# An input quantizer whose small steps are done once for four batches

## The reference

```
x = (h - mean) / sqrt(var + 1e-5)              # 2560 rows of 512
chunks of 64 rows:                             # 10 for each batch, 40 in all
ch_bias = (max + min) / 2                      # per chunk and channel
xz = x - ch_bias
tmax = max |xz| of the chunk; cmax = max |xz| of the chunk and channel
idx = sum(cmax > tmax / 2**(7..1))             # 8 scale groups of channels
scale = tmax / 2**(7 - idx) / 7
result = clip(round(xz / scale), -8, 7) * scale
q, k, v = result @ W_quantized + ch_bias @ W + b
```

## Time and profile before

| | |
|---|---|
| time, median of 3 runs | 1826.13 us (1821.69 to 1829.0) |
| the profiled execution | 1825.29 us, of which the span of the trace is 1823.5 us |
| busy shares in the span | PE 74%, DVE 72%, ACT 42%, POOL 27% |
| TensorE's mean granted clock | 0.864 of full speed |
| stretch of the normalisation and quantizer | 166.9 to 292.6 us |

### The profile page before, as it was taken

One profiled execution on the slowest core, in us unless ns is written; L12 is line 12 of the kernel. 1 busy time (PEld: TensorE's weight loads), 2 busy tenths in 40 slices (PEclk: granted clock), 3 DMA queues, 4 the chain that ended last, 5 costly groups with the idle time before them and its releaser, 6 DMA issues. The chain is left out here.

```text
span 1823.5 us, 30220 instructions
## 1 busy us (share of the span) xinstructions
PE 1341.7 (74%) x10126; PEld 766.5 (42%) x10245; DVE 1309.7 (72%) x2158; ACT 767.5 (42%) x1459; POOL 500.1 (27%) x313
## 2 busy tenths in 40 slices
PE   0366117864989999999999941426469999999993
PEld 0335103321334444344444410113457777777772
DVE  7975898996878888788888819999644444444441
ACT  4565001330667777677777740002213333333331
POOL 4000113764134343343300002123113233333321
PEclk9976559785899999999999975667579999999997
DMA  4002002769457767667564443326458887878865
GB/s 146 1 0 84 0 0 78 222 210 210 148 168 200 209 181 210 183 185 209 162 123 77 107 137 82 68 34 177 152 211 283 269 289 258 264 266 289 260 166 138
DMA packets 115662, 294.31 MB, mean 161 GB/s; under 512 B 19772, under 2 KB 54332, under 8 KB 105446
## 3 DMA queue, kind: packets, MB, share of 16 engines
q1 hardware_dynamic: 89262, 205.79, 36.9%
q0 software_dynamic: 25280, 84.95, 17.7%
q10 hardware_dynamic: 1056, 2.79, 0.5%
HBM read 206.39 MB, written 92.16 MB: 164 GB/s over the span
## 5 line engine op out<-in xcount | busy, mean ns | idle before, releaser
L1292 ACT ACTIVATE pT<-p 128x512 f32<-128x512 f32 x800 | 421.6, 607 | 170.8 <-PE p L1194 97.5
L1266 DVE TENSOR_REDUCE mxa<-p 128x1 f32<-128x512 f32 x640 | 409.3, 682 | 99.0 <-PE p L1176 98.8
L1176 PE MATMUL p<-ks,qs 96*128 96x512 bf16 x640 | 253.8, 399 | 34.7 <-DMA vs<-d_v 27.1
L1194 PE MATMUL p<-qs,ks 128*128 128x512 bf16 x560 | 215.2, 384 | 26.3 <-DMA qs<-nmT 13.0
L1212 PE MATMUL p<-pT,vs 128*32 128x128 f32 (+1 forms) x2560 | 207.1, 441 | 1.4 <-ACT pT L1292 1.4
L1812 PE MATMUL p<-x,w 128*128 128x256 bf16 x1728 | 191.6, 273 | 0.0
L1812 PEld LDWEIGHTS p<-x,w 128*128 128x128 bf16 x1728 | 169.1, 98 | 23.4
L1783 POOL DMA_INDIRECT d_acc<-yo,slot_row x54 | 86.5, 1602 | 311.2 <-DMA d_acc<-yo,slot_row 260.6
L1891 DVE SCALAR_TENSOR_TENSOR sg<-p,b,sg 128x256 f32<-128x256 f32 x108 | 52.3, 484 | 118.3 <-ACT sg L1857 118.2
L1212 PEld LDWEIGHTS p<-pT,vs 128*32 128x32 f32 x2560 | 67.0, 109 | 153.2 <-issue 109.9
L1147 POOL CAST xT<-xT 128x2048 bf16<-128x2048 f32 x24 | 45.3, 1887 | 300.7 <-PE p L1212 288.5
(11 more groups left out here) (333 smaller groups left out, 2117.8 us busy)
## 6 DMA issues: line engine op xcount, KB each, us to landing
w<-d_w SPq DMA_DIRECT2D x18, 2048.0 KB, 8.5
d_w<-xT POOLq DMA_DIRECT2D x24, 1024.0 KB, 6.4
shared<-d_w SPq DMA_DIRECT2D x9, 2048.0 KB, 8.3
w<-d_w SPq DMA_DIRECT2D x18, 1024.0 KB, 7.2
xT<-in_w1T POOLq DMA_DIRECT2D x16, 1024.0 KB, 10.6
qs<-d_q SPq DMA_DIRECT2D x192, 80.0 KB, 3.6
ks<-d_k SPq DMA_DIRECT2D x192, 80.0 KB, 3.7
d_v<-xT SPq DMA_DIRECT2D x20, 512.0 KB, 4.4
```

Source lines behind the costliest of these rows:

```text
L1176: mm = pe.matmul(out, qs[u][0:STACK, h, q], ks[u][0:STACK, h, 0:512], start=True, stop=True)
L1194: mm = pe.matmul(out, ks[u][:, h, k], qs[u][:, h, 0:512], start=True, stop=True)
L1266: dve.tensor_reduce(mxa[u][:, h, qt:qt + 1], bank, AX.X, ALU.max, negate=True).then_inc(s_mfree, 1)
L1292: act.activation(dst, ps[:, second_bank(c, s)], ACT.Exp).then_inc(s_p, 1)
```

## The change

A new class `GroupQuantizer` takes the place of `Quantizer` in `project`. The ORDER list goes. Now:

- DVE takes the statistics of all four batches' first tiles in a row, one square root serves all 20 tiles, and 20 tiles are normalised one after the other. PE's transposes use four PSUM banks.
- `extremes` (DVE, for each batch) does maximum, minimum and the negated chunk bias. GpSimd adds it to batches 0, 1 and 2 (`centre`), ACT to batch 3 in 40 activations of 128x64 with the bias as a per-partition operand.
- `scales` (DVE, once) does the small operations on 128x160 values for all 40 chunks, with one round trip over PE. The scale group no longer comes from the loop of seven comparisons: it comes from the exponent and mantissa bits of the maxima, taken as integers.
- `apply` (DVE, for each batch) multiplies, rounds, and clamps; the last pass is four instructions of 128x640 instead of one of 128x2560.
- the token scales are copied by ACT, and the bias products use the negated bias, which the following operation subtracts.

```
+    def extremes(self, dve, chain, b, x):
+        at = self.columns(b)
+        chain(dve.tensor_reduce(self.mx[:, :, at], self.chunks(x), AX.X, ALU.max))
+        chain(dve.tensor_reduce(self.mn[:, :, at], self.chunks(x), AX.X, ALU.min))
+        chain(dve.tensor_tensor(self.ncb[:, :, at], self.mx[:, :, at], self.mn[:, :, at], ALU.add))
+        dve.tensor_scalar(self.ncb[:, :, at], self.ncb[:, :, at], -0.5, None, ALU.mult).then_inc(self.bias_ready, 1)
+    def scales(self, dve, chain, k, ready):
+        chain(dve.tensor_tensor(self.mx[:], self.mx[:], self.ncb[:], ALU.add))
+        chain(dve.tensor_tensor(self.mn[:], self.mn[:], self.ncb[:], ALU.add))
+        chain(dve.scalar_tensor_tensor(self.u[:], self.mn[:], -1.0, self.mx[:], ALU.mult, ALU.max))
+        dve.tensor_reduce(self.c1[:], self.u[:].rearrange("p i c -> p c i"), AX.X, ALU.max).then_inc(self.cmax_ready, 1)
+        dve.wait_ge(self.cmax_turned, k + 1)
+        chain(dve.tensor_reduce(self.tm[:], self.ps_t[0:n, 0:P], AX.X, ALU.max))
+        dve.tensor_scalar(self.diag[:], self.ident[0:n, 0:n], self.tm[:], None, ALU.mult).then_inc(self.tmax_ready, 1)
+        dve.wait_ge(self.tmax_spread, k + 1)
+        chain(dve.tensor_copy(self.tmb[:], self.ps_b[:, 0:n]))
+        chain(dve.scalar_tensor_tensor(self.up[:], wide(self.tmb[:]), 2.0 ** -7, self.u[:], ALU.mult, ALU.max))
+        chain(dve.tensor_scalar(bits(self.tf[:]), bits(self.tmb[:]), MANTISSA, UNITY, ALU.bitwise_and, ALU.bitwise_or))
+        chain(dve.tensor_scalar(bits(self.F[:]), bits(self.up[:]), MANTISSA, UNITY, ALU.bitwise_and, ALU.bitwise_or))
+        chain(dve.tensor_scalar(bits(self.tp[:]), bits(self.tmb[:]), EXPONENT, None, ALU.bitwise_and))
+        chain(dve.tensor_scalar(bits(self.s[:]), bits(self.up[:]), EXPONENT, None, ALU.bitwise_and))
+        chain(dve.tensor_scalar(bits(self.tp[:]), bits(self.tp[:]), -1.0, float(2 * UNITY), ALU.mult, ALU.add))
+        chain(dve.tensor_tensor(self.F[:], self.F[:], wide(self.tf[:]), ALU.is_gt))
+        chain(dve.scalar_tensor_tensor(self.F[:], self.F[:], 1.0, self.s[:], ALU.add, ALU.mult))
+        chain(dve.tensor_tensor(self.F[:], self.F[:], wide(self.tp[:]), ALU.mult))
+        chain(dve.tensor_tensor(self.s[:], self.F[:], wide(self.tmb[:]), ALU.mult))
+        chain(dve.tensor_scalar(self.s[:], self.s[:], 1.0 / QMAX, 1e-9, ALU.mult, ALU.max))
+        dve.tensor_scalar(self.gb[:], self.tmb[:], 1.0 / QMAX, 1e-9, ALU.mult, ALU.max).then_inc(ready, 1)
+        dve.wait_ge(ready, k + 1)
+        chain(dve.reciprocal(self.rg[:], self.gb[:]))
+        chain(dve.tensor_tensor(self.F[:], self.s[:], wide(self.rg[:]), ALU.mult))
+        chain(dve.reciprocal(self.s[:], self.s[:]))
+    def apply(self, dve, chain, b, x, out, done):
+        chain(dve.tensor_tensor(x4, x4, self.spread(self.s[:, :, at]), ALU.mult))
+        chain(dve.tensor_scalar(flat, flat, MAGIC, MAGIC, ALU.add, ALU.subtract))
+        for i in range(IT):
+            ins = dve.scalar_tensor_tensor(o4[:, i], x4[:, i], QMAX, self.F[:, i, at].unsqueeze(2).broadcast_to(
+                [P, self.NB, CHUNK]), ALU.min, ALU.mult)
+        ins.then_inc(done, 1)
...
@@ ACT: after one square root and 20 copies
+            act.wait_ge(quant.bias_ready, B)
+            for i in range(IT):
+                for c in range(NB):
+                    x = xT[:, LAST, i, c * CHUNK:(c + 1) * CHUNK]
+                    ins = act.activation(x, x, ACT.Identity, bias=quant.ncb[:, i, k:k + 1])
+            ins.then_inc(s_centred[1], 1)
+            act.wait_ge(s_scales, 1)
+            for half in range(2):
+                act.copy(gtok[rows], g[rows, :, half]).then_inc(s_gtok, 1)
@@ GpSimd
-            for b in range(B):
-                quant.gpsimd(pool, b, xT[:, b])
+            for b in range(LAST):
+                pool.wait_ge(quant.bias_ready, b + 1)
+                quant.centre(pool, b, xT[:, b]).then_inc(s_centred[0], 1)
@@ DVE
+            for b in range(B):
+                ins = dve.bn_stats(bst[:, b], hs[:, b * COMPS])
+            chain(ins)
+            for b in range(B):
+                ins = dve.bn_aggr(mv[:, b * COMPS], bst[:, b])
+            chain(ins)
+            dve.tensor_scalar(mv[:, :, 1], mv[:, :, 1], EPS_LN, None, ALU.add).then_inc(s_var, 1)
+            dve.wait_ge(s_std, 1)
+            chain(dve.reciprocal(sd[:], sd[:]))
+            for r in range(TILES):
+                b, c = divmod(r, COMPS)
+                if b >= 2 and c == 0:
+                    dve.wait_ge(s_turn, (b - 1) * COMPS)
+                dve.tensor_scalar(xn[:, b % 2, c], hs[:, r], mv[:, r, 0:1], sd[:, r:r + 1],
+                                  ALU.subtract, ALU.mult).then_inc(s_xn, 1)
+            for b in range(B):
+                dve.wait_ge(s_xT, (b + 1) * COMPS)
+                quant.extremes(dve, chain, b, xT[:, b])
+            dve.wait_ge(quant.bias_ready, B)
+            quant.scales(dve, chain, 0, s_scales)
+            for b in range(B):
+                if b < LAST:
+                    dve.wait_ge(s_centred[0], b + 1)
+                else:
+                    dve.wait_ge(s_centred[1], 1)
+                quant.apply(dve, chain, b, xT[:, b], qF[:, b], s_q)
...
+            dve.wait_ge(s_gtok, 2)
```

More of the change, by code:

```diff
@@ L743, in vector, with __init__, sb, sem @@
         dve.scalar_tensor_tensor(o3, x3, QMAX, wide(self.F[:]), ALU.min, ALU.mult).then_inc(done, 1)
-    def token_scales(self, dve, chain):
-        g = self.gb[:].rearrange("p b (t h) -> p (b t) h", h=2)
-        for half in range(2):
-            rows = slice(half * CHUNK, (half + 1) * CHUNK)
-            chain(dve.tensor_copy(self.gtok[rows], g[rows, :, half]))
+class GroupQuantizer:
+    NB = T // CHUNK
+    def __init__(self, nc, ctx, ident, ones, ps_t, ps_b, tag, batches):
+        def sb(name, shape, dt=F32):
+            return ctx.enter_context(nc.sbuf_tensor(f"{name}{tag}", shape, dt))
+        def sem(name):
+            return ctx.enter_context(nc.semaphore(f"{name}{tag}"))
+        self.n = n = batches * self.NB
+        self.ident, self.ones, self.ps_t, self.ps_b = ident, ones, ps_t, ps_b
+        self.mx, self.mn, self.u, self.up, self.F, self.s, self.ncb = (sb(x, [P, IT, n]) for x in (
+            "qmx", "qmn", "qu", "qup", "qF", "qs", "qncb"))
+        self.c1, self.tmb, self.tf, self.tp, self.gb, self.rg = (sb(x, [P, n]) for x in (
+            "qc1", "qtmb", "qtf", "qtp", "qgb", "qrg"))
+        self.tm, self.diag = sb("qtm", [n, 1]), sb("qdiag", [n, n])
+        self.bias_ready, self.cmax_ready, self.cmax_turned, self.tmax_ready, self.tmax_spread = (sem(x) for x in (
+            "chunk_bias_ready", "chunk_max_ready", "chunk_max_turned", "tmax_ready", "tmax_spread"))
+    def tensor(self, pe, k):
+        n = self.n
+        pe.wait_ge(self.cmax_ready, k + 1)
+        pe.transpose(self.ps_t[0:n, 0:P], self.c1[:], self.ident[:]).then_inc(self.cmax_turned, 1)
+        pe.wait_ge(self.tmax_ready, k + 1)
+        pe.matmul(self.ps_b[:, 0:n], self.ones[0:n, :], self.diag[:], start=True, stop=True).then_inc(self.tmax_spread, 1)
+    def columns(self, b):
+        return slice(b * self.NB, (b + 1) * self.NB)
+    def spread(self, ap):
+        return ap.unsqueeze(3).broadcast_to([P, IT, self.NB, CHUNK])
+    def chunks(self, x):
+        return x.rearrange("p i (c t) -> p i c t", c=self.NB)
+    def centre(self, eng, b, x):
+        return eng.tensor_tensor(self.chunks(x), self.chunks(x), self.spread(self.ncb[:, :, self.columns(b)]), ALU.add)
+    def extremes(self, dve, chain, b, x):
[5 more added lines that the diff above has]
+    def scales(self, dve, chain, k, ready):
+        n = self.n
+        EXPONENT, MANTISSA, UNITY = 0x7F800000, 0x007FFFFF, 0x3F800000
+        def bits(ap):
+            return ap.bitcast(I32)
+        def wide(ap):
+            return ap.unsqueeze(1).broadcast_to([P, IT, n])
+        chain(dve.tensor_tensor(self.mx[:], self.mx[:], self.ncb[:], ALU.add))
[24 more added lines that the diff above has]
+    def apply(self, dve, chain, b, x, out, done):
+        at = self.columns(b)
+        x4 = self.chunks(x)
+        flat = x.rearrange("p i t -> p (i t)")
+        chain(dve.tensor_tensor(x4, x4, self.spread(self.s[:, :, at]), ALU.mult))
+        chain(dve.tensor_scalar(flat, flat, MAGIC, MAGIC, ALU.add, ALU.subtract))
+        o4 = self.chunks(out)
+        for i in range(IT):
+            ins = dve.scalar_tensor_tensor(o4[:, i], x4[:, i], QMAX, self.F[:, i, at].unsqueeze(2).broadcast_to(
+                [P, self.NB, CHUNK]), ALU.min, ALU.mult)
+        ins.then_inc(done, 1)
@@ L956, in _ @@
                 dve.wait_ge(s_bmm, n + 1)
[L957 removed]
+                dve.tensor_tensor(Bt[:, n], bias[:, n], ps[0:NCH, n], ALU.subtract).then_inc(s_bt, 1)
             for n in range(2):
```

73 lines of the change are left out of this document (28 added, 45 removed).

## The result

The changed kernel takes 1786.34 us (median of 5 runs, 1773.3 to 1788.99), the kernel before 1826.13 in the same comparison: a ratio of 0.977, with a 95% interval of 0.975 to 0.979. Two further sets of five gave 1782.58 (1773.83 to 1786.19; ratio 0.977, 0.974 to 0.979) and 1779.89 (1776.56 to 1783.6; ratio 0.974, 0.971 to 0.977). The forecast was 1781 in a range of 1775 to 1797. The profiled execution of the changed kernel is the quickest of its set: 1773.3 us, span 1771.3.

The account below looks back on a forecast made before the run. VectorE (DVE) was taken to bound the changed stretch: 120.1 us becomes 14.3 + 24.5 + 9.1 + 29.4 = 77.3, and 1.98 goes at the end, 44.8 less in all, giving 1781 us, range 1775 to 1797.

Parts of the forecast that it names:

- The normalisation: First statistic to last normalised tile in `project`: 14.3 us, 12.9 to 15.5 depending on when PE's clock rises.
- The extremes: Maximum, minimum and bias on DVE, unchanged at 6.12 us a batch, 24.5 in all.
- The reductions beside GpSimd: DVE's reductions during GpSimd's centring in `extremes`: delay taken as 0, bounds 0 and 13.1 us.
- the first rival: GpSimd holds off DVE's reductions in `extremes`: 13.1 us more, 1794; chance 0.09.
- the second rival: GpSimd's centring gets longer from its bias's access pattern: at 9 us, 10 more, 1791; chance 0.05.
- the third: ACT's centring of batch 3 comes late: at 1 us per activation 9 more, 1790; chance 0.01.
- The scales: Small operations done once for all 40 chunks, with one PE round trip and 18 gaps: 9.1 us.
- The end: Two copies of L750 leave DVE before the products: 1.98 us less, bound 0.2 if the memset holds an operation.
- The sum: Changed stretch up to the products: 120.1 us becomes 77.3, 42.8 less, plus 1.98 at the end, 44.8.
- the lock: In the old quantizer, DVE's subtraction L717 is held off while GpSimd centres: 4 x 4.36 = 17.4 us.
- The other stages: Stages outside the changed stretch keep their lengths within 2 us; the product loop starts at PE's low clock as before.
- Slower than before: Expert stage gets a lower granted clock after the shift: at 0.88, 58 us more, 1839; chance 0.02.

Follow-up runs that it names:

- the spare multiplications: 24 matmuls with unread results, keeping TensorE busy ahead of the product loop, added to the changed kernel: 1771.05 us, again 1773.25 (0.970 of the kernel before both times).
- ScalarE centring: The kernel before, with ScalarE instead of GpSimd centring all four batches: 1816.5 us, ratio 0.995.

## Where the prediction was right, and where its terms were off

*What bounds the stretch.* VectorE, before and after, as predicted; the length of the stretch is its operations, one behind the other.

*The normalisation*, forecast 14.3 (12.9 to 15.5), took 12.83 (167.24 to 180.07), the lower bound, and 12.8 to 13.5 over the eleven profiles of the changed kernel and its variants. TensorE's granted clock went to 1.00 at 7.4 us after the first statistic: the 18 copies behind the second one took 9.07 us, 0.50 apart, and no longer 0.85, so VectorE waited for no tile. The middle value was too high: every one of the eleven lies below it.

*The extremes*, forecast 24.5, took 24.3. *The reductions beside GpSimd* were the one unknown with a price of 13.1, set at 0, and were 0 (2.81 and 2.82). The Trainium skill ("SBUF — State Buffer", Who interferes with whom) says that on trn2 `tensor_reduce` never contends with GpSimd, and the trace of after agrees (2.81 beside it, 2.82 alone). The addition after the minimum stayed at 0.20.

So the first rival is out. *GpSimd's centring* took 4.48, and 4.47 before: the second rival is out. *ScalarE's centring* took 9.65 of the 12.1 allowed and ended 21 us ahead of its use: the third is out.

*The scales*, forecast 9.1, took 9.0. A wide operation took 0.33, as priced; those on bits 0.18 to 0.24, a little less; the strided reduction of L813 took 0.43 instead of 0.33.

*The passes*, forecast 29.4, took 29.3 (213.34 to 242.67).

*The end*, forecast 1.98 less, gave 2.4 less: from the end of the passes to the first product 2.7 us, and 5.1 before. The memset held nothing.

*The sum*, 44.8 in the stretch, was 47.1; 1.5 of the difference is the clock in the normalisation. By kind: the lock 16.6, and not 17.4, since the four operations would have taken 0.20 each without it; the other small operations 23.2, from 4 x (12.2 - 4.16) = 32.2 to 9.0, which is a reading of the two traces and no run of its own; the normalisation 5.0, from 120.1 - 4 x 25.58 (177.75 to 203.33) = 17.8 to 12.8; the end 2.4; the extremes 0.2; and the passes 0.5 the other way. That the whole time came near the forecast is in part luck: the stretch gave 2.3 more than the sum, the product loop took 1.9 that the sum did not have, and the two all but cancel (45.2 for 44.8).

*The other stages* keep their lengths within 2 us: nearly so, and not by the reason given. The product loop lost 1.9, and the prediction called it a loop that "starts with PE at the low clock as before". It started lower for longer: 4.42 us for 16 products, against 3.26 for 15 before, and the granted clock rose at 4.4 us behind the first product, against 2.3 before. In the changed kernel the bias products are done early and TensorE then stands idle for 23.3 us. The prediction saw that they had time to spare, and not that the clock at the start of the loop could change by it. That the loop's length goes with this clock is shown by the spare multiplications (2.6 to 3.6 us). That the early bias products are the reason is not shown: with ScalarE centring they stood late, and the loop was as long.

*Slower than before:* `experts` took 458.5 us and 458.7 before, and the granted clock of the stage was 0.97 in both. This rival is out.

*The Trainium skill's advice* ("ScalarE: Activation LUTs", Rules for kernel authors) to leave additions to VectorE holds for the work in itself: a batch takes 9.65 us on ScalarE, and a pass of VectorE over as much data 2.82. It does not hold for the sum, since VectorE is the path and ScalarE has the time. Against GpSimd, which takes 4.48, the slow way gained 4.1 us here and 9.0 in the kernel before, since it takes GpSimd's lock off VectorE.

## What to carry to other kernels

Where GpSimd and VectorE share a stretch, look at which VectorE operations stand beside GpSimd's: put reductions there and two-tensor operations elsewhere. It gave 12.5 us here. Small operations cost by their number (0.20 us for 40 elements, 0.33 for 160): done once for four batches they gave 23 us. And when work is moved ahead of a dense loop of TensorE, look at the granted clock at which the loop now starts: it was worth 2 to 4 us here, in a loop that VectorE bounds.
